# A fused transformer block on one core: first keys gathered in halves by two queues, x loaded first, the value bias moved into the residual, and no score maxima for a fifth chunk

## The chip, the cores and the metric

The kernel runs on one core of one Trainium2 chip. Its engines are TensorE (PE; PEld is its weight load), VectorE (DVE), ScalarE (ACT), GpSimd (POOL) and SyncE (SP); a name with a q behind it (SPq, ACTq) is that engine's queue of instructions, from which it also issues DMAs. The metric is device time in microseconds (us), the median of several executions.

## The reference

```python
x = x + cross_attention(layernorm(x), ctx, ctx, tau, delta)   # softmax(E**-0.5 * (q k^T tau + delta_s)) v, 16 heads of E = 16
x = x + expert_ffn(layernorm(x))                              # 8 experts, the best one by the router, times its probability
x = x + window_attention(ctx, layernorm(x), len, p_t)         # keys p_t - 16 .. p_t + 16, gauss weights, tanh(cat @ W_c^T)
x = x + slot_layer(layernorm(x))                              # top 8 of 64 slots per token, GRU and attention over the slots
```

x has 2048 tokens of 256 channels, ctx has 1601 rows of 256. Queries, keys, values and the output of the first attention are projections of 256 by 256 with a bias each: q = Wq x + bq, k = Wk c + bk, v = Wv c + bv, and the result is out @ Wo^T + bo. Everything is float32.

## The kernel before

The tokens are worked off in 4 chunks (`NC`) of 512 (`CT`). The 16 heads form 4 groups (`NG`) of 4 (`HG`), the 1601 context rows 13 tiles (`ST`).

**The stacks.** Scores come from one bf16 product over 101 rows: q and k are each split into three bf16 parts whose products are stacked over 6 times 16 rows (`PART_OF_ROW`), three rows carry the three parts of delta against ones, and two rows carry the negated maximum of each token against ones. The parts are made in blocks of 128 channels by up to 512 columns (`BLOCKS`: `("K", i, m)`, `("Q", i, m)`). For a block, PE projects (`project`, L829), ACT writes the float32 copy (L666) and the high part (L672), and the first 6 blocks are then split on DVE (`split`, L1220, L1222, L1224), the later ones by POOL and ACT (L606, L678, L613). SP's queue then gathers the stack rows: `gather_k(g)` moves 6 times 16 partitions of 4 heads by 1601 columns (L473), `first_q(g)` the same for q (L482).

**Three stretches.** (1) `START`: loads, K blocks 0 to 3 of the first 128 channels, both Q blocks of chunk 0, and 8 of the 13 value tiles (`V`, L904 on PE, L1254 on DVE, which adds the bias bv). The normalised x that the Q blocks need comes from `stats` on DVE, `scale_shift` on POOL (L580 to L590) and L697 on ACT. (2) `UNITS + LEAD` = 78 maximum units, with the remaining blocks laid between them by the list `BESIDE` (pairs of a unit's number and a step, the same list walked by every engine). A unit is one product of 99 rows by 401 columns (`max_unit`, L869) and one DVE maximum over it (`take_max`, L1292); 64 units give the maxima of one group of heads for one chunk. Three PSUM banks (`RING`) hold units in flight. (3) Four chunks of 52 slots (`SLOTS`), a slot being one tile of context rows for one group of heads: 4 score products (L1152), 4 exponentials on ACT (L719), 4 value products (`pv`, L948), and 4 or 5 maximum units for what comes 78 units later. Everything else of the previous chunk (`behind(c - 1)`: output projection, experts, window attention, slots) is laid between the slots by a fixed table of places (`AT`). After the last slot `behind(3)` and the slot layer run alone.

In the fourth chunk the units of the third stretch run on past the last group: units 1024 to 1101 are maxima for a fifth chunk, from queries that SP has copied behind the stored ones:

```python
sp.dma_start(q_parts[:, :, T:T + CT], q_parts[:, :, 0:CT]).then_inc(s["q0_copied"], 16)
```

The maxima come into the query stack as two rows (`load_m`, L492). For the first group SP issues them behind all the query stores:

```python
for i in range(1, NC):
    for m in range(KT):
        store_q(i, m)
wait_taken(sp, "m", 0)
load_m(0)
```

In each chunk `chunk_loads` lets SP load the next maxima and queries, and, in its fourth step, store the previous chunk's residual and load x for this chunk into `xres` (L547), to which POOL adds the bias bo (L639).

## Time and profile before

| | us |
|---|---|
| median of 3 runs (lowest, highest) | 1152.18 (1151.59, 1152.73) |
| the profiled execution's own time | 1152.93 |
| its span in the profile | 1151.2 |
| PE busy, share of the span | 1017.0, 88% |
| DVE busy | 790.4, 69% |
| ACT busy | 576.1, 50% |
| first maximum unit starts on PE | 48.28 |
| first score product of the third stretch | 119.95 |
| last score product | 1012.52 |

Busy time is a union: a matmul counts from its start to its modelled end, so matmuls that overlap are counted once, and a PE busy all the time isn't a PE at its peak. In the rows, `out<-in` names the tensors; the brackets at the end of a timeline row give the idle time of the engine before it and what ended it. Where a tensor shares the memory of another, the profile uses the other's name (`q_stack<-q_stack` is the split of delta, `expert_w` holds the projection weights early on, `xres` the ones).

### The profile page before, as it was taken

The page shows a single profiled execution, that of the slowest core. Times are in us where ns is not written, and L with a number is a line of the kernel's source. Part 1 is how long each engine was busy: PE and PEld are TensorE (multiplying, and loading weights), DVE is VectorE, ACT ScalarE, POOL GpSimd, SP SyncE. Part 2 cuts the span into 40 slices and gives each one's busy share as a digit, 9 for nine tenths or more (in the row PEclk, how much of TensorE's full clock was granted, in tenths as well). Part 3 has the DMA queues.
Part 4 walks back from the last instruction along what each step waited for, and adds up shares of the span by engine and source line. Part 5 has one row for each costly group of instructions (what it writes and reads, how often), then busy time and mean ns, then how long its engine had stood idle before and what let it go on. Part 6 is the DMA issues. An engine that isn't in the chain of part 4 may idle for free.

```text
span 1151.2 us, 13842 instructions
## 1 busy us (share of the span) xinstructions
PE 1017.0 (88%) x4890; PEld 410.2 (36%) x4890; DVE 790.4 (69%) x1772; ACT 576.1 (50%) x1047; POOL 68.3 (6%) x86
## 2 busy tenths in 40 slices
PE   5677899999899998989889999888999989889887
PEld 2333222222333333433333334323333334344544
DVE  3487678788766778676777767776677787735444
ACT  4144566666544556665445546664444465720120
POOL 5143000000100000000000000001000000010000
PEclk8889899999989999999899989999999899999999
DMA  4981700000100000001000000010000000050022
GB/s 127 154 167 56 170 15 1 15 15 3 30 1 15 1 15 1 15 1 52 1 15 1 14 1 15 1 38 14 15 1 3 12 1 15 1 165 1 1 91 73
DMA packets 35746, 38.28 MB, mean 33 GB/s; under 512 B 6943, under 2 KB 32320, under 8 KB 35416
## 3 DMA queue, kind: packets, MB, share of 16 engines
q1 hardware_dynamic: 34988, 36.83, 13.0%
q8 instruction: 39, 0.64, 0.2%
q0 software_dynamic: 80, 0.26, 0.2%
q10 hardware_dynamic: 608, 0.30, 0.1%
q14 instruction: 31, 0.25, 0.1%
HBM read 23.49 MB, written 8.13 MB: 27 GB/s over the span
## 4 chain that ended last, share of the span: by engine, by line
issue 45%; PE 30%; DVE 11%; DMA 4%; ACT 3%; SPq 3%; DVEq 2%; POOL 2%; POOLq 1%; ACTq 0%
PE ps_o L948 8%; PE ps_e L1152 8%; PE ps_m L869 7%; DVE mx L1292 6%; DMA xres<-in_x 1%; SPq L436 1%; PE ps_e L829 1%; ACT probs L719 1%; PE ps_m L1096 1%; PE ps_m L1099 1%; DMA x<-xres 1%; POOL xres L639 1%; DVE xn L1284 1%; POOL rstd L582 1%; PE ps_m L1003 1%
## 5 line engine op out<-in xcount | busy, mean ns | idle before, releaser
L1292 DVE TENSOR_REDUCE mx<-ps_m 128x1 f32<-128x401 f32 x1102 | 580.6, 568 | 235.6 <-PE ps_m L869 227.7
L719 ACT ACTIVATE probs<-ps_e 128x512 f32<-128x512 f32 (+1 forms) x832 | 472.7, 597 | 374.2 <-PE ps_e L1152 373.2
L869 PE MATMUL ps_m<-k_stack,q_stack 99*128 99x401 bf16 x1102 | 343.8, 344 | 50.6 <-DVE mx L1292 41.2
L1152 PE MATMUL ps_e<-q_stack,k_stack 101*128 101x512 bf16 (+1 forms) x832 | 327.1, 393 | 14.9 <-DMA q_stack<-mrow 6.6
L948 PE MATMUL ps_o<-probs,v_heads 128*32 128x512 f32 (+1 forms) x1664 | 228.4, 622 | 0.0
L1152 PEld LDWEIGHTS ps_e<-q_stack,k_stack 101*128 101x128 bf16 (+1 forms) x832 | 82.8, 100 | 310.2 <-ACT probs L719 205.4
L869 PEld LDWEIGHTS ps_m<-k_stack,q_stack 99*128 99x128 bf16 x1102 | 110.2, 100 | 177.0 <-DVE mx L1292 112.8
L1046 PE MATMUL ps_m<-expert_w,xnT 128*128 128x512 f32 x256 | 130.1, 609 | 16.3 <-DVE xb L1428 16.3
L1428 DVE SCALAR_TENSOR_TENSOR xb<-ps_m,hot,xb 128x256 f32<-128x256 f32 x112 | 54.2, 484 | 18.0 <-PE ps_m L1046 9.0
L1046 PEld LDWEIGHTS ps_m<-expert_w,xnT 128*128 128x128 f32 x256 | 47.1, 194 | 47.9 <-DVE xb L1428 24.7
L948 PEld LDWEIGHTS ps_o<-probs,v_heads 128*32 128x32 f32 (+1 forms) x1664 | 33.2, 109 | 65.7 <-issue 57.3
L580 POOL TENSOR_TENSOR var_e<-mv,eps 128x4 f32<-128x4 f32 x16 | 3.2, 200 | 654.6 <-DVE mv L1377 647.1
L729 ACT COPY xnT<-ps_m 128x512 f32<-128x512 f32 x24 | 13.8, 587 | 48.1 <-PE ps_m L993 48.1
L968 PE MATMUL ps_m<-wc,ident 128*128 128x512 f32 x64 | 29.6, 602 | 0.8 <-ACT alphaT L788 0.8
L639 POOL TENSOR_TENSOR xres<-xres,bo 128x1024 f32<-128x1024 f32 x4 | 9.4, 2356 | 312.2 <-DMA xres<-in_x 312.2
L829 PE MATMUL ps_e<-probs,expert_w 128*128 128x512 f32 (+1 forms) x32 | 19.0, 722 | 7.9 <-DMA probs<-in_ctxT 7.9
L829 PE MATMUL ps_e<-xnT,expert_w 128*128 128x512 f32 x32 | 20.9, 759 | 1.7 <-issue 1.7
L1096 PE MATMUL ps_m<-win_v,work 128*128 128x256 f32 x64 | 19.6, 399 | 2.0 <-ACT work L729 2.0
L993 PE MATMUL ps_m<-ident,xn 128*128 128x128 f32 x96 | 18.5, 291 | 2.9 <-DVE xn L1284 2.7
L666 ACT ACTIVATE work<-ps_e,cond 128x512 f32<-128x512 f32 (+1 forms) x8 | 4.7, 592 | 29.5 <-PE ps_e L829 29.5
L1099 PE MATMUL ps_m<-wc,xnT 128*128 128x256 f32 x64 | 19.3, 394 | 0.0
L666 ACT ACTIVATE work<-ps_e,cond,tau 128x512 f32<-128x512 f32 x8 | 6.2, 778 | 24.0 <-PE ps_e L829 24.0
(236 smaller groups left out, 650.6 us busy)
## 6 DMA issues: line engine op xcount, KB each, us to landing
q_stack<-q_parts SPq DMA_DIRECT2D x96, 64.0 KB, 2.5
k_stack<-k_stack SPq DMA_DIRECT2D x12, 200.1 KB, 8.6
expert_w<-in_expert_wT SPq DMA_DIRECT2D x2, 1024.0 KB, 10.5
xres<-in_x SPq DMA_DIRECT2D x4, 512.0 KB, 3.9
x<-xres SPq DMA_DIRECT2D x4, 512.0 KB, 3.2
probs<-x SPq DMA_DIRECT2D x1, 2048.0 KB, 8.3
out<-probs SPq DMA_DIRECT2D x4, 512.0 KB, 3.0
k_stack<-alphaT SPq DMA_DIRECT2D x10, 200.1 KB, 8.1
```

The costliest lines, as they stand in the source:

```text
L639: pool.tensor_tensor(xres[:], xres[:], bo0[:].unsqueeze(1).broadcast_to((P, TT, D)), ALU.add)\
L719: act.activation(probs[0:n, k % 2, h, :], ps_e[h % 2][0:n, :], ACT.Exp).then_inc(s["exp_done"], 1)
L829: mm = pe.matmul(ps_e[b % 2][:, 0:n], wqkv[:, w, k, P * m:P * m + P], src[:, k, at_col:at_col + n], start=(k == 0), stop=(k == KT - 1))
L869: pe.matmul(ps_m[:, (UNITS * n1 + u) % RING, 0:SPLIT], qst[0:MAX_ROW, g, h, P * t:P * t + P], kst[0:MAX_ROW, HG * g + h, QUARTER_START[q]: ...
L948: mm = pe.matmul(ps_o[32 * h:32 * h + 32, :], v_sb[0:n, st, HG * g + h, :], probs[0:n, k % 2, h, :], start=(st == 0), stop=(st == ST - 1))
L968: pe.matmul(out, ident[:], wc[:, 0:KT, :], start=True, stop=True)
L1046: mm = pe.matmul(bank(name, c), xnT[:, k, P * t:P * t + P], expert_w[:, k, CT * j:CT * j + CT], start=(k == 0), stop=(k == KT - 1))
L1096: pe.matmul(o, aT[:, k, tok:tok + P], win_v[:, k, :], start=(k == 0), stop=False)
L1099: mm = pe.matmul(o, xnT[:, k, tok:tok + P], wc[:, KT + k, :], start=False, stop=(k == KT - 1))
L1152: pe.matmul(ps_e[h % 2][0:n, :], kst[0:ROWS, HG * g + h, P * st:P * st + n], qst[0:ROWS, g, h, :], start=True, stop=True).then_inc(s["qk_r ...
L1292: dve.tensor_reduce(mx[:, q, col:col + 1], ps_m[:, (UNITS * n1 + u) % RING, 0:SPLIT], AX.X, ALU.max)\
L1428: last = dve.scalar_tensor_tensor(out=xb[:, t, :], in0=bank(f"e{i}", c)[:, D * (e % 2):D * (e % 2) + D], scalar=hot8[:, t, e:e + 1], in1=( ...
```

## The change

- **Loads.** x's first chunk goes first on SP's queue, Wq third, x's second chunk before all waits. The bias bv is no longer loaded; Wo comes with the constants.
- **Delta.** It is laid out over 13 partitions of 128 and split by DVE. The three parts go out to memory and come back spread over 12 heads in one DMA; the ones come in 2 DMAs in place of 6.
- **Order of the start.** DVE takes x's statistics before the conditions, POOL the scale and shift before its window load. Ten products of ones run on PE ahead of everything (`WARM`). tau is multiplied into Wq (`S`), no longer applied by ACT. `("Q", 0, 1)` and three value tiles move from `START` to `BESIDE`, whose pieces lie 2 units apart in place of 2.4 and number 36 in place of 31.
- **Gathers.** The first group's keys move in two halves of columns, each when its blocks are split, rows 0, 4, 2 by SP and rows 1, 5, 3 by ACT; its queries likewise. The gathers of groups 2 and 3 both come behind all query stores.
- **Early split.** For the first 5 blocks DVE reads PSUM itself and adds the bias; ACT's float32 copy is left out.
- **Values.** ACT copies the value tiles. PE forms bv @ Wo^T in 4 matmuls on a broadcast bv, and DVE adds that to bo.
- **Maxima.** `load_m(0)` is issued by ACT. Units from 1024 on, their transposes, the copy of the queries, and the loads of queries for a fifth chunk are left out. `xres` is loaded after the store of the previous chunk's residual without waiting for the maxima of a group 16, but with a wait until its last readers on DVE are through.

```diff
-EARLY = N_COLS + 2
-V_EARLY = 8
-START = [("D",), ("C",), ("L", 0), ("K", 0, 0), ("K", 1, 0), ("N", 0), ("K", 2, 0), ("T", 0), ("K", 3, 0), ("Q", 0, 0), ("Q", 0, 1)]
+EARLY = N_COLS + 1
+V_EARLY = 5
+HALVES = ((0, 2 * CT, 1), (2 * CT, S, N_COLS - 1))
+GATHER_SP, GATHER_ACT = (0, 4, 2), (1, 5, 3)
+START = [("D",), ("L", 0), ("C",), ("K", 0, 0), ("N", 0), ("S",), ("K", 1, 0), ("T", 0), ("K", 2, 0), ("K", 3, 0), ("G", 0),
+         ("Q", 0, 0), ("G", 1), ("g",)]
...
+SPACE = 2
+WARM = 10
...
-BESIDE += [(76, ("P", "Q", 3, 1))]
+BESIDE += [(SPACE * len(PIECES) + 2, ("P", "Q", 3, 1)), (UNITS + 8, ("m",))]
...
+def wanted(n1):
+    return n1 < NG * NC
...
+            sp.dma_start(xa[:], x_dram[:, 0:TT, :]).then_inc(x_start[0], 16)
             load_w(0, "L0_WkT")
             load_ctx(0)
-            sp.dma_start(xa[:], x_dram[:, 0:TT, :]).then_inc(x_start[0], 16)
...
+            sp.dma_start(d_parts.rearrange("a (p s) -> p a s", s=P), delta3[:]).then_inc(s["delta_stored"], 16)
+            sp.wait_ge(s["delta_stored"], 16)
+            sp.dma_start(kst[DELTA_ROW:DELTA_ROW + 3, 0:3 * HG, :], d_parts[:, 0:S].unsqueeze(1).broadcast_to((3, 3 * HG, S)))\
+              .then_inc(s["ld_delta_k"], 16)
...
-            gather_k(0)
-            sp.wait_ge(s["ld_delta_k"], 48)
-            first_q(0)
-            sp.dma_start(xb[:], x_dram[:, TT:2 * TT, :]).then_inc(x_start[1], 16)
+            rows = range(K_PARTS)
+            for first_col, end_col, last_block in HALVES:
+                sp.wait_ge(s["blk_parts"], BLOCK["K", last_block, 0] + 1)
+                move_k(sp, 0, GATHER_SP, first_col, end_col)
+            sp.wait_ge(s["blk_parts"], BLOCK["Q", 0, 0] + 1)
+            move_q(sp, 0, GATHER_SP)
+            move_q(sp, 1, rows)
+            store_q(0, 0)
...
-            wait_taken(sp, "m", 0)
-            load_m(0)
+            move_k(sp, 2, rows)
...
                 for g in range(NG):
-                    wait_taken(sp, "m", NG * c + g + 1)
-                    load_m((g + 1) % NG)
-                    load_q(sp, (g + 3) % NG, c if g == 0 else c + 1)
-                    if g == NG - 1:
-                        if behind:
-                            store_x3(c - 1)
-                            sp.wait_ge(s["x3_stored"], 16 * c)
-
-                        sp.dma_start(xres[:], x_dram[:, c * TT:c * TT + TT, :]).then_inc(s["x_loaded"], 16)
+                    if wanted(NG * c + g + 1):
+                        wait_taken(sp, "m", NG * c + g + 1)
+                        load_m(sp, (g + 1) % NG)
+                    if g == 0 or c < NC - 1:
+                        load_q(sp, (g + 3) % NG, c if g == 0 else c + 1)
+                if behind:
+                    store_x3(c - 1)
+                    sp.wait_ge(s["x3_stored"], 16 * c)
+                    sp.wait_ge(s["xn_ready"], NC + 3 * c)
+                sp.dma_start(xres[:], x_dram[:, c * TT:c * TT + TT, :]).then_inc(s["x_loaded"], 16)
...
-            pool.wait_ge(s["delta_hi"], 1)
-            pool.tensor_tensor(delta_b, delta_a, delta3[:, 0, :], ALU.subtract)
...
+                if b >= EARLY:
+                    act.wait_ge(s["blk_rest"], b - 1)
+                    act.activation(q32[:, b % 2, 0:n], ps_e[b % 2][:, 0:n], ACT.Identity, bias=bias)
...
+                if kind == "m":
+                    wait_taken(act, "m", 0)
+                    load_m(act, 0)
...
+                    for k in range(KT):
+                        mm = pe.matmul(ps_x[:, W:W + D], bv_rows[:, k, :], wo_rows[:, k, :], start=(k == 0), stop=(k == KT - 1))
...
                         for j, u in units_at(k, h):
-                            max_unit(u, c, j)
+                            if wanted(NG * c + j):
+                                max_unit(u, c, j)
```

## Rows read from the trace of the kernel before

**Rows 1.** Stretches: start:end length, busy PE PEld DVE ACT POOL, clock, DMA share, GB/s
```profile
0.00:48.20 48.20, 24.90 (x64) 14.06 (x64) 19.56 (x47) 14.45 (x20) 17.19 (x21) 0.88 0.66 120
48.20:114.40 66.20, 50.33 (x183) 25.71 (x183) 51.45 (x122) 27.47 (x46) 25.27 (x34) 0.88 0.58 131
...
944.20:1013.50 69.30, 62.76 (x348) 25.95 (x348) 51.20 (x122) 43.60 (x78) 1.21 (x2) 1.00 0.04 10
```
**Rows 2.** Timeline of the start: start us, us, engine line operation
```profile
6.62 3.75 PE L829 MATMUL ps_e<-probs,expert_w 128*128 128x512 f32 x4 [6.62 <-DMA probs<-in_ctxT]
17.97 0.19 POOL L580 TENSOR_TENSOR var_e<-mv,eps 128x4 f32<-128x4 f32 x1 [5.75 <-issue]
25.46 3.28 POOL L625 TENSOR_TENSOR q_stack<-expert_w,q_stack 16x1601 bf16<-16x1601 f32 x1
31.13 4.59 SPq L473 DMA_DIRECT2D k_stack<-k_stack  x6
35.85 4.31 SPq L482 DMA_DIRECT2D q_stack<-probs  x6
48.28 0.50 PE L869 MATMUL ps_m<-k_stack,q_stack 99*128 99x401 bf16 x1 [8.07 <-DMA q_stack<-probs]
```
**Rows 3.** Timeline of early blocks: DVE's operations, one of them slow, and ACT's norm
```profile
11.77 0.69 DVE L1220 TENSOR_TENSOR work<-work,k_stack 128x512 f32<-128x512 f32 x1 [0.35 <-ACT k_stack L672]
12.55 0.43 DVE L1222 CAST k_stack<-work 128x512 bf16<-128x512 f32 x1
13.05 0.69 DVE L1224 TENSOR_TENSOR k_stack<-work,k_stack 128x512 bf16<-128x512 f32 x1
20.74 2.07 ACT L697 ACTIVATE xn<-xa,off,rstd 128x256 f32<-128x256 f32 x4 [3.99 <-POOL off L590]
25.95 3.07 DVE L1222 CAST k_stack<-work 128x512 bf16<-128x512 f32 x1
```
**Rows 4.** Stretches by DMA rate, the last column: first gather, constants
```profile
36.00:40.00 4.00, 4.00 (x20) 3.36 (x18) 1.86 (x5) 0.00 (x0) 0.00 (x0) 1.00 1.06 116
48.00:52.00 4.00, 3.72 (x7) 1.76 (x8) 1.63 (x3) 0.00 (x0) 0.00 (x0) 0.50 1.10 342
```
**Rows 5.** Groups of instructions from 48.2 to 114.4 us, PE and DVE
```profile
L904 PE MATMUL ps_o<-expert_w,probs 128*128 128x256 f32 (+1 forms) x20 | 5.3, 385 | 0.0
L1254 DVE TENSOR_TENSOR v_heads<-ps_o,scratch 128x256 f32<-128x256 f32 (+1 forms) x5 | 2.1, 413 | 0.0
```
**Rows 6.** Timeline between the last of the 78 units and the first score product
```profile
117.03 1.21 SPq L492 DMA_DIRECT2D q_stack<-mrow  x2
119.95 0.58 PE L1152 MATMUL ps_e<-q_stack,k_stack 101*128 101x512 bf16 x1 [6.63 <-DMA q_stack<-mrow]
```
**Rows 7.** The maximum products among the groups from 944.2 to 1013.5 us
```profile
L869 PE MATMUL ps_m<-k_stack,q_stack 99*128 99x401 bf16 x79 | 24.3, 336 | 4.2 <-DVE mx L1292 4.1
```
**Rows 8.** Timeline of PE in one slot of chunk 0
```profile
224.19 0.51 PE L869 MATMUL ps_m<-k_stack,q_stack 99*128 99x401 bf16 x2
225.20 0.39 PE L1152 MATMUL ps_e<-q_stack,k_stack 101*128 101x512 bf16 x1
225.69 1.07 PE L948 MATMUL ps_o<-probs,v_heads 128*32 128x512 f32 x8
```
**Rows 9.** Stretches within the last 16 slots
```profile
947.90:966.60 18.70, 18.29 (x104) 9.66 (x103) 11.38 (x22) 10.75 (x19) 0.00 (x0) 1.00 0.09 22
966.60:982.30 15.70, 13.88 (x78) 4.83 (x77) 14.06 (x35) 9.49 (x18) 1.21 (x2) 1.00 0.00 1
993.50:1013.50 20.00, 16.96 (x89) 5.01 (x91) 15.87 (x45) 11.93 (x25) 0.00 (x0) 1.00 0.06 12
```
**Rows 10.** Timeline behind the last slot: x and the first residual
```profile
1017.82 0.38 SPq L547 DMA_DIRECT2D xres<-in_x  x1
1019.47 3.69 PE L1003 MATMUL ps_m<-wo_rows,attn_chunk 128*128 128x256 f32 x16 [0.77 <-ACT attn_chunk L729]
1021.79 2.35 POOL L639 TENSOR_TENSOR xres<-xres,bo 128x1024 f32<-128x1024 f32 x1 [44.87 <-DMA xres<-in_x]
```

More of the change, by code:

```diff
@@ L156, in job_numbers @@
                 order += [(name, c - 1) for name in AT if AT[name] == q]
-            if q in M_AT:
+            if q in M_AT and wanted(NG * c + 1 + M_AT.index(q)):
                 order.append(("m", NG * c + 1 + M_AT.index(q)))
@@ L429, in block_cols, with k_loads, move_k, move_q @@
             return k_cols[BLOCKS[b][1]][1] if BLOCKS[b][0] == "K" else CT
+        def k_loads(g):
+            return K_PARTS * (2 if g == 0 else 1) + (g == 3)
+        def move_k(eng, g, rows, first_col=0, end_col=S):
+            m, first = g * HG // (P // E), g * HG % (P // E)
+            for j in rows:
+                eng.dma_start(kst[16 * j:16 * j + 16, HG * g:HG * g + HG, first_col:end_col],
+                              k_part[m][PART_OF_ROW[j]][E * first:E * (first + HG), first_col:end_col]).then_inc(k_loaded[g], 16)
+        def move_q(eng, g, rows):
+            m, first = g * HG // (P // E), g * HG % (P // E)
+            for j in rows:
+                part = [a for start, a, copies in PART_GROUPS for _ in range(copies)][j]
+                eng.dma_start(qst[16 * j:16 * j + 16, g, :, :], q_part[m][E * first:E * (first + HG), part, :])\
+                   .then_inc(q_loaded[g], 16)
+        def load_m(eng, g):
+            for a in range(2):
+                eng.dma_start(qst[MAX_ROW + a:MAX_ROW + a + 1, g, :, :], mrow[:, a, :]).then_inc(m_loaded[g], 16)
         def load_q(eng, g, chunk):
@@ L476, in first_q @@
-            def first_q(g):
-                m, first = g * HG // (P // E), g * HG % (P // E)
-                sp.wait_ge(s["blk_parts"], BLOCK["Q", 0, m] + 1)
-                for j, a, copies in PART_GROUPS:
-                    for i in range(copies):
-                        sp.dma_start(qst[16 * (j + i):16 * (j + i) + 16, g, :, :], q_part[m][E * first:E * (first + HG), a, :])\
-                          .then_inc(q_loaded[g], 16)
+            sp.dma_start(d_parts.rearrange("a (p s) -> p a s", s=P), delta3[:]).then_inc(s["delta_stored"], 16)
@@ L501, in _ @@
                 sp.dma_start(dst, src).then_inc(s["ld_const"], 16)
-            gather_k(1)
-            first_q(1)
-            first_q(2)
-            for m in range(KT):
-                store_q(0, m)
+            store_q(0, 1)
+            move_q(sp, 2, rows)
+            move_k(sp, 1, rows)
             sp.wait_ge(s["xnT_ready"], 2)
             sp.dma_start(xb[:], x_dram[:, 3 * TT:4 * TT, :]).then_inc(x_start[1], 16)
-            gather_k(2)
             for i in range(1, NC):
@@ L662, in block_hi @@
                 n = block_cols(b)
-                bias, scale = (qk_bias[:, 1, :], 1.0) if kind == "K" else (qk_bias[:, 0, :], tau[:, 2:3])
+                bias = qk_bias[:, kind == "K", m:m + 1]
                 act.wait_ge(s["blk_psum"], b + 1)
-                need(act, s["blk_rest"], b - 1)
-                act.activation(q32[:, b % 2, 0:n], ps_e[b % 2][:, 0:n], ACT.Identity, bias=bias[:, m:m + 1], scale=scale)
+                if b >= EARLY:
+                    act.wait_ge(s["blk_rest"], b - 1)
+                    act.activation(q32[:, b % 2, 0:n], ps_e[b % 2][:, 0:n], ACT.Identity, bias=bias)
                 if kind == "Q":
@@ L920, in _ @@
             under_way = []
+            pe.wait_ge(s["consts_set"], 1)
+            for _ in range(WARM):
+                pe.matmul(ps_o[:], ones_sb[:, 0:P], ones_sb[:, 0:CT], start=True, stop=True)
             for now in START:
                 if now == ("T", 0):
-                    pe.wait_ge(s["ld_early"], 32)
+                    pe.wait_ge(s["ld_early"], 16)
                 step(*now)
                 finish()
-            pe.wait_ge(s["ld_k"], 32)
-            pe.wait_ge(s["ld_delta_k"], 48)
-            pe.wait_ge(s["ld_ones"], 16 * NG)
+            pe.wait_ge(s["ld_k"], 16)
+            pe.wait_ge(s["ld_delta_k"], 16)
+            pe.wait_ge(s["ld_ones"], 16)
             pe.wait_ge(s["v_taken"], V_EARLY)
@@ L1316, in step @@
                     stats((xa, xb)[i % 2])
[L1317 to L1321 removed]
+                if kind == "D":
+                    split_delta()
                 if kind == "C":
                     condition()
+                if kind == "S":
+                    dve.wait_ge(w_loaded[2], 16)
+                    dve.tensor_scalar(wqkv[:, 2], wqkv[:, 2], tau[:, 2:3], None, ALU.mult).then_inc(s["wq_scaled"], 1)
                 if kind == "U":
@@ L1532, in chunk @@
                         go_on(work, HG * k + h)
-                        if h == 2 and max_end(k - 1) is not None:
+                        if h == 2 and max_end(k - 1) is not None and wanted(NG * c + max_end(k - 1)):
                             j = max_end(k - 1)
```

163 lines of the change are left out of this document (83 added, 80 removed), and 8 rows, old and new, of the table PIECES.

## The prediction

> **What bounds the kernel now.** I read the table of stretches first, cut where the work changes [rows 1]. The first 48.2 us feed PE for 24.9 us only: nothing of the main work has begun. From 48.2 to 114.4 neither engine is full: PE is busy 50.3 us of 66.2, DVE 51.5, and they wait for each other through three PSUM banks. From 114.4 to 119.9 PE does nothing [rows 6]. Then come four chunks of slots, of which the diff alters only the last 16 slots, from 944.2 to 1013.5 us, where PE is busy 62.8 us of 69.3. Behind them runs a serial end. So four places count: when the first maximum unit can start, how long the 78 units take, the hole behind them, and the last 16 slots with what follows.
>
> The timeline of the start shows what the first unit (48.28) waited for [rows 2]. SP gathers the keys only from 31.13, after POOL's last delta part (25.46 + 3.28 = 28.74) and three DMAs for it; six key DMAs take 4.59 us to issue, six query DMAs end their issue at 35.85 + 4.31 = 40.16, and PE is released by the last query landing, 8 us later. That is no latency but a backlog: while it lasts the DMA share is full (1.06), yet only 116 GB/s move, against 342 when constants come from memory [rows 4].
>
> **Part 1, the start.** x (512 KB) goes ahead of Wk and the first context columns. At 342 GB/s it costs 1.5 us, so the first K block starts near 8.2 instead of 6.62 [rows 2, 4]. The ten products of ones lie before it, in PE's idle time; whether they make the first block's 3.75 us into half I can't see in this trace, and it matters by 1.9 us at most. x itself is there some 3 us sooner, and POOL takes its scale and shift before its window load. With statistics ending near 8.5 and a POOL chain of 2.8 us (17.97 to 20.74, [rows 2, 3]), ACT's normalisation (2.07 us) ends near 13.4 where it ended at 22.8 [rows 3].
>
> From there DVE paces. A block costs it 0.69 + 0.43 + 0.69 us and two drains, 2.05 us [rows 3]. The third block's cast took 3.07 us instead of 0.43 while POOL worked on delta [rows 2, 3]; with delta in 13 partitions on DVE that overlap is gone. ACT spends one pass per block, not two. I lay it out: K block 0 split by 12.9, K block 1 by 16.3 (ACT gives it the high part after the normalisation), block 2 by 19.1, the short block 3 by 19.9, the query block by 22.3. SP, which had waited for delta's round trip through memory behind 3.4 MB of loads (about 16 to 17 us at 342 GB/s, [rows 4]), issues the first key half from about 17.2, the second from 19.9, its query rows from 22.3 to 24.2; ACT does the same with 1 us delay. tau into Wq is one DVE pass below 0.7 us, before K block 1 has its high part.
>
> The gathers move 1.2 MB of keys and 0.4 MB of queries, with delta 1.74 MB. At the 116 GB/s of [rows 4] this takes 15.0 us from 17.2: 32.2, and with the landing and group 1's queries, which share the engines, 33.5. If the two queues get more out of the DMA engines, the limit is the last issue at 24.2 plus 2.2 to 2.9 us: 27. SP and ACT take row groups 16 partitions apart, which spreads the writes; but the nearest row is the slow one, so I take 31. That is 17.3 us before 48.28 [rows 2].
>
> The Trainium skill says otherwise (DMA: Bandwidth & Descriptors, section "Issuing engines are not separate DMA queues"): DMAs of several issuers interleave on the same 16 engines, and a second issuer saves only the time of issuing. By it the first unit would start near 33.5. No run here shows two queues gathering at once.
>
> **Part 2, the 78 units.** Added on PE: one query block, half of the 3.75 us of [rows 2] at the higher clock, 1.9; three value tiles, 1.06 each by 5.3 / 5 [rows 5]; four small products for bv @ Wo, 0.9. Together 6.0 us. Off DVE go five value additions, 2.1 us [rows 5]; on it come a broadcast copy and one addition, 0.8. ACT takes eight value copies, about 0.4 us each; it is busy 27.5 us of 66.2 [rows 1], which hides them. The normalisations are asked for 7 units ahead of their transposes, not 4; I credit 4 us of PE's idle time for that, of 15.9 us (66.2 - 50.3) in all. Of the 6.0 us added, part falls into gaps of PE: the stretch goes from 66.2 to 68 us, with bounds of 62 (all hidden, waits gone) and 73 (all added, nothing gained). It ends at 31 + 68 = 99.
>
> **Part 3, the hole.** PE's first score product waits 6.63 us for the rows of maxima, which SP issues at 117.03 behind the last query store [rows 6]. ACT will issue them right after its last high part, before the last split. Left are two issues of 0.6 us and 1.7 to 2.2 us of landing from about the 73rd unit on, that is 1 to 1.5 us behind the last unit. The third stretch starts near 100.2 instead of 119.95: 19.7 us saved. What is late next is nothing I can find. Groups 2 and 3 of the keys are now gathered behind all query stores, 12 DMAs at 4.59 us per six [rows 2], landed by about 125; the first unit that reads group 2 is the 50th of the third stretch, at 4 to 5 units per slot its tenth slot, beyond 130. ACT's exponentials wait for the split and the last store of channel half 0, as now.
>
> **Part 4, the last 16 slots.** 78 units go, with one turn of maxima. On PE the 79 products show 24.3 us busy [rows 7], which is the upper bound. But products overlap: two in a row show 0.51 us, one 0.34 [rows 7, 8], so one more costs 0.17, and 78 cost 13.3. The lower bound is the one unit that lies between a slot's last score product and its value products: 0.49 us between their starts, 0.22 left without it [rows 8], 0.27 x 16 = 4.3, if ACT's exponentials and the two banks hold everything else in place. By parts [rows 9]: 947.9 to 966.6 is PE-bound (18.29 of 18.7), some 20 units less, 3.4 us. 966.6 to 982.3 is DVE-bound (14.06 of 15.7); without its maxima DVE has some 3.5 us of work there, PE 13.88 - 3.4 = 10.5, ACT 9.5: 3.1 us. 993.5 to 1013.5: PE 16.96 - 3.6, ACT 11.9: 2.6 us. The other 14.9 us (69.3 less these three) hold ACT's table loads around the gelu: 2.1 us for 17 units. Sum 11.2 us.
>
> **Part 5, behind the last slot.** x for chunk 3 is issued at 1017.82, behind the useless maxima and queries of a fifth chunk, POOL adds bo from 1021.79 to 1024.14, while PE has both halves of the projection done at 1023.16 [rows 10]. With the load issued after the previous residual's store, tens of us earlier, DVE begins at the first half and ends its second addition near 23.8 instead of 25.45: 1.7 us, carried through, for the chain behind is serial. The new wait for the residual's readers is over in every chunk before its x is wanted.
>
> **Sum.** 19.7 + 11.2 + 1.7 = 32.6 us. From the span of 1151.2 to 1118.6, from the execution's own 1152.93 to 1120.3; it lies 0.75 above the median of the runs, so 1119.6.
>
> **The rivals.**
> - *One rate for both queues* (by the rule above): the gathers stay at 116 GB/s and the first unit waits to 33.5. For it: the full share at 116 GB/s in [rows 4]. Against: the share says busy engines, not used ones. 2.5 us more: 1122.1. Chance 0.25.
> - *Freed PE time isn't usable.* The last slots keep their pace because exponential and score product alternate on two banks; 4.3 us in place of 11.2, and the 78 units take 73: 1119.6 + 6.9 + 5 = 1131.5. For it: ACT idles in those slots waiting for PE, and PE for it. Chance 0.13.
> - *The maximum units cost what they show.* 24.3 us in the last slots, 1106.5. Against: the overlap in [rows 8]. For it: DVE is the pace of two of the parts [rows 9]. Chance 0.1.
> - *Slower: the clock.* With a third of PE's work gone in the last 16 slots the granted clock could fall from 1.00 there [rows 1] to half and stay. PE's 62.8 - 13.3 = 49.5 us would become 99 us, 29.7 more than the 69.3 now, 41 more than forecast: 1160. It decides only if nearly all 16 slots run at half, from about 33 us of extra time on. Against: in the 78-unit stretch PE is busy 76% and still has 0.88, and [rows 9] shows 1.00 at 85%. Chance 0.02.
> - *The edits buy nothing*, because another wait stands in the same places (SP behind delta's round trip until the old time, 31.13, and a late group 2): about 1150. Chance 0.01.
>
> **How the numbers follow.** The forecast, 1119.6, has 0.49. Its own range is 1115 to 1124: the start of the first unit between 27 and 33.5, the units between 65 and 71. The range to give reaches to the neighbours: 1108 to 1130 leaves out the worst of the second rival, the full price of the third, and the last two. Faster by over 0.2% (2.3 us, about what a measurement of this kernel can tell from no change): 0.97. Within: 0.01. Slower: 0.02.
>
> **What would show it.** First maximum unit at 27 to 34 us, with a DMA rate in the gather above or at 116 GB/s; K block 1 split by 16 to 17; normalised x near 13. 78 units in 62 to 73 us. The first score product within 2 us of the last unit's end. Slots of the last quarter at about 3.6 us in place of 4.3, the clock still 1.00. x's load for chunk 3 before 1000 us, and no wait for POOL behind the last slot. The prediction is wrong if the start is held by a DMA that I haven't counted (delta and ones now lie on few partitions and so on few DMA engines), if the units need over 73 us, or if the last slots gain less than 5 us.

## The result, and the profile after

| | before | after |
|---|---|---|
| median, us (lowest to highest, 4 runs each) | 1152.31 (1151.59 to 1152.73) | 1119.32 (1118.38 to 1120.53) |
| ratio after / before, 95% interval | | 0.9729 [0.9697, 0.9761] |
| the profiled execution's own time | 1152.93 | 1120.53 |
| its span | 1151.2 | 1118.8 |
| first maximum unit on PE | 48.28 | 35.81 |
| first score product of the third stretch | 119.95 | 98.07 |
| PE busy | 1017.0 | 1008.3 |

The change takes 33 us off, 2.7%, which is what was forecast. The profile says that two of the terms were nevertheless wrong, in opposite directions. To see it, cut the execution after at the same events as before and read the stretches; columns as in [rows 1]. Later on, "the last 16 slots" runs from the first exponential of slot 36 of the fourth chunk to the end of the last exponential: 944.2 to 1013.5 before [rows 1], 920.4 to 983.1 after.

```profile
0.00:35.80 35.80, 22.55 (x60) 11.44 (x60) 12.78 (x40) 9.38 (x18) 8.91 (x18) 0.92 0.85 181
35.80:97.60 61.80, 51.91 (x201) 28.68 (x201) 49.03 (x117) 31.17 (x58) 27.58 (x37) 0.93 0.45 111
...
920.40:983.10 62.70, 55.73 (x269) 19.89 (x271) 11.35 (x42) 42.94 (x79) 3.56 (x3) 0.86 0.06 18
98.50:920.40 821.90, 762.87 (x3900) 280.02 (x3899) 611.32 (x1329) 469.82 (x862) 16.88 (x20) 0.97 0.07 17
983.10:1118.80 135.70, 114.69 (x400) 63.17 (x392) 56.63 (x153) 20.09 (x42) 4.42 (x8) 0.95 0.19 60
```

Lined up with the forecast (minus is time saved, in us of the span; "before" takes the first exponential at 120.6 as the end of the start, "after" at 98.5):

| stretch | forecast | profile after | from |
|---|---|---|---|
| start, units and hole, up to the third stretch | -19.7 | -22.1 | 120.6 to 98.5 |
| the first 192 slots | 0 | -1.7 | 823.6 to 821.9 |
| the last 16 slots | -11.2 | -6.6 | 69.3 to 62.7 |
| behind them | -1.7 | -2.0 | 137.7 to 135.7 |
| sum | -32.6 | -32.4 | 1151.2 to 1118.8 |

**The start.** The timeline of the changed kernel (PE, DVE, ACT and the two queues):

```profile
2.81 4.44 PE L957 MATMUL ps_o<-xres 16*128 16x512 bf16 x10 [2.81 <-POOL xres L589]
8.74 5.89 PE L861 MATMUL ps_e<-probs,expert_w 128*128 128x512 f32 x8 [1.49 <-DMA probs<-in_ctxT]
...
12.60 0.69 ACT L683 ACTIVATE k_stack<-ps_e,cond 128x512 bf16<-128x512 f32 x1 [7.69 <-PE ps_e L861]
...
13.19 2.06 ACT L728 ACTIVATE xn<-xa,off,rstd 128x256 f32<-128x256 f32 x4
...
14.67 0.69 DVE L1264 TENSOR_TENSOR k_stack<-work,k_stack 128x512 bf16<-128x512 f32 x1
...
17.20 0.69 DVE L1264 TENSOR_TENSOR k_stack<-work,k_stack 128x512 bf16<-128x512 f32 x1
...
18.30 0.24 SPq L503 DMA_DIRECT2D k_stack<-d_parts  x1
...
18.59 5.37 SPq L451 DMA_DIRECT2D k_stack<-k_stack  x6
19.33 1.84 ACTq L451 DMA_DIRECT2D k_stack<-k_stack  x2
...
19.83 1.96 PE L861 MATMUL ps_e<-xnT,expert_w 128*128 128x512 f32 x4 [1.26 <-DVE work L1259]
...
24.61 6.09 SPq L459 DMA_DIRECT2D q_stack<-probs  x9
...
35.81 0.52 PE L901 MATMUL ps_m<-k_stack,q_stack 99*128 99x401 bf16 x1 [3.24 <-DMA q_stack<-probs]
```

Normalised x is there by 13.19 + 2.06 = 15.3 (forecast 13.4, before 22.8): ACT makes the high part of K block 0 first, and for that it waits until 12.60 for PE. K block 1 is split at 17.9 (forecast 16.3), the first half is issued at 18.6 (17.2), right behind the DMA of delta's rows, whose way through memory had held SP until 18.3, the queries at 24.6 (22.3), and PE is still released by a query row, 11.2 us after that issue. The stretches by DMA rate show what lies between:

```profile
8.00:12.00 4.00, 3.25 (x4) 1.51 (x5) 1.54 (x17) 0.00 (x0) 1.82 (x5) 1.00 1.08 375
...
20.00:24.00 4.00, 4.00 (x16) 2.77 (x15) 2.81 (x8) 0.69 (x1) 0.00 (x0) 1.00 1.07 146
24.00:28.00 4.00, 1.03 (x4) 0.59 (x3) 0.58 (x1) 0.93 (x3) 0.00 (x0) 0.86 1.08 131
28.00:32.00 4.00, 3.28 (x10) 2.21 (x8) 0.00 (x0) 0.74 (x2) 0.00 (x0) 0.72 1.15 145
32.00:36.00 4.00, 0.76 (x3) 0.13 (x2) 0.00 (x0) 0.00 (x0) 0.00 (x0) 0.71 1.13 209
```

Loads from memory move 375 GB/s (first row). The share is as full afterwards, but 131 to 146 GB/s move while the first group's rows are on their way, little more than the 116 of [rows 4]; the 209 of the last row already hold loads from memory again.

**The hole.** ACT issues the rows of maxima before the last unit, and PE waits 0.34 us where it waited 6.63 [rows 6]:

```profile
94.47 0.58 ACTq L464 DMA_DIRECT2D q_stack<-mrow  x1
95.08 0.61 ACTq L464 DMA_DIRECT2D q_stack<-mrow  x1
...
98.07 0.38 PE L1189 MATMUL ps_e<-q_stack,k_stack 101*128 101x512 bf16 x1 [0.34 <-DMA q_stack<-mrow]
```

**The last 16 slots.** In the stretches above PE's clock is 0.86 there, where [rows 1] had 1.00. Finer stretches show where it goes:

```profile
956.00:960.00 4.00, 3.80 (x20) 1.64 (x20) 0.00 (x0) 3.46 (x5) 0.00 (x0) 1.00 0.00 0
960.00:962.00 2.00, 1.04 (x8) 0.97 (x8) 0.00 (x0) 1.97 (x3) 0.00 (x0) 1.00 0.03 8
962.00:966.00 4.00, 3.19 (x12) 0.54 (x12) 2.75 (x16) 2.38 (x5) 0.00 (x0) 0.51 0.00 0
...
974.00:978.00 4.00, 3.68 (x14) 0.83 (x14) 0.42 (x1) 2.17 (x4) 0.00 (x0) 0.50 0.00 0
978.00:982.00 4.00, 4.00 (x17) 0.90 (x9) 0.00 (x0) 1.52 (x3) 0.00 (x0) 0.85 0.00 0
```

From 962.5 to 979.5 the granted clock is 0.50, the lower of its two levels, 1.2 GHz. What PE did before: at 960 to 962 it was busy half of the time, behind ACT's table loads for the gelu. Slots 47 to 51, from 962.2 on, take 20.9 us against 20.0 before, although they have lost their units; the eleven slots ahead of them take 41.8 against 49.3. That is the rival of the clock, in small.

**Behind them.** x for chunk 3 is loaded at 947.5 and has its bias long before DVE wants it at 991, so no wait for POOL is left:

```profile
947.52 0.37 SPq L564 DMA_DIRECT2D xres<-in_x  x1
951.30 2.35 POOL L650 TENSOR_TENSOR xres<-xres,bo 128x1024 f32<-128x1024 f32 x1 [5.29 <-DMA xres<-in_x]
...
988.92 3.69 PE L1040 MATMUL ps_m<-wo_rows,attn_chunk 128*128 128x256 f32 x16 [0.77 <-ACT attn_chunk L760]
990.99 0.69 DVE L1409 TENSOR_TENSOR xa<-xres,ps_m 128x512 f32<-128x512 f32 x1 [3.99 <-PE ps_m L1040]
992.65 0.69 DVE L1409 TENSOR_TENSOR xa<-xres,ps_m 128x512 f32<-128x512 f32 x1 [0.97 <-PE ps_m L1040]
```

### The profile page after: what moved, and what is told of

Read it like the earlier page. It is cut to its first block, busy times and chain, and to the rows that moved or that the text cites. A ratio compares the mean times of both kernels' runs of the same rounds, so it can differ in the third digit from the quotient of the medians.

```text
span 1118.8 us, 13600 instructions
## 1 busy us (share of the span) xinstructions
PE 1008.3 (90%) x4825; PEld 403.5 (36%) x4825; DVE 742.0 (66%) x1681; ACT 573.4 (51%) x1056; POOL 62.3 (6%) x85
## 4 chain that ended last, share of the span: by engine, by line
issue 52%; PE 28%; DVE 9%; DMA 4%; ACT 2%; POOL 2%; DVEq 2%; SPq 1%; POOLq 0%; ACTq 0%
PE ps_e L1189 7%; PE ps_o L985 7%; PE ps_m L901 6%; DVE mx L1335 4%; PE ps_e L861 2%; DMA xres<-in_x 1%; SPq L471 1%; POOL rstd L599 1%; DMA q_stack<-probs 1%; POOL xres L650 1%; ACT probs L750 1%; DVE xn L1327 1%; PE ps_m L1133 1%; PE ps_m L1136 1%; PE ps_m L1248 1%
## 5 line engine op out<-in xcount | busy, mean ns | idle before, releaser
L1335 DVE TENSOR_REDUCE mx<-ps_m 128x1 f32<-128x401 f32 x1024 | 539.4, 569 | 212.3 <-PE ps_m L901 204.1
L901 PE MATMUL ps_m<-k_stack,q_stack 99*128 99x401 bf16 x1024 | 319.1, 343 | 34.4 <-DVE mx L1335 29.7
L985 PE MATMUL ps_o<-probs,v_heads 128*32 128x512 f32 (+1 forms) x1664 | 231.7, 630 | 0.0
L901 PEld LDWEIGHTS ps_m<-k_stack,q_stack 99*128 99x128 bf16 x1024 | 102.3, 100 | 150.8 <-DVE mx L1335 90.9
L1083 PE MATMUL ps_m<-expert_w,xnT 128*128 128x512 f32 x256 | 129.1, 605 | 16.3 <-DVE xb L1472 16.3
L1083 PEld LDWEIGHTS ps_m<-expert_w,xnT 128*128 128x128 f32 x256 | 46.7, 193 | 47.4 <-DVE xb L1472 24.7
L1519 DVE TENSOR_TENSOR xres<-xb,work 128x512 f32<-128x512 f32 x8 | 5.5, 687 | 22.4 <-ACT work L803 22.4
L677 ACT ACTIVATE work<-ps_e,cond 128x512 f32<-128x512 f32 (+1 forms) x11 | 7.2, 653 | 22.2 <-PE ps_e L861 22.2
L1040 PE MATMUL ps_m<-win_k,xnT 128*128 128x256 f32 x64 | 16.2, 383 | 2.2 <-issue 1.4
```

The source lines that it names most:

```text
L901: pe.matmul(ps_m[:, (UNITS * n1 + u) % RING, 0:SPLIT], qst[0:MAX_ROW, g, h, P * t:P * t + P], kst[0:MAX_ROW, HG * g + h, QUARTER_START[q]: ...
L985: mm = pe.matmul(ps_o[32 * h:32 * h + 32, :], v_sb[0:n, st, HG * g + h, :], probs[0:n, k % 2, h, :], start=(st == 0), stop=(st == ST - 1))
L1083: mm = pe.matmul(bank(name, c), xnT[:, k, P * t:P * t + P], expert_w[:, k, CT * j:CT * j + CT], start=(k == 0), stop=(k == KT - 1))
L1335: dve.tensor_reduce(mx[:, q, col:col + 1], ps_m[:, (UNITS * n1 + u) % RING, 0:SPLIT], AX.X, ALU.max)\
```

## The experiments

Each kernel is the changed kernel with the edit shown, run beside the kernel before on the same chip, on one of two chips. Times spread more there: the kernel before took 1144.3 to 1156.5, and the changed kernel, on one of them, 1114.6 to 1121.2. So times are read as ratios to before with their intervals, and most verdicts rest on stretches of the profile. The changed kernel's own ratio is 0.9729 [0.9697, 0.9761] above and 0.9735 [0.9709, 0.9762] in a second measurement there (its profile is read further down). Each edit has one profile. What two profiles of the same work can differ by is seen in those whose edit leaves a stretch alone: the first unit comes between 35.3 and 37.1 us, and the 78 units take 58.2 to 63.5 us from the first one's start to the last one's.

**The fifth chunk's maxima put back.**

```diff
 def wanted(n1):
-    return n1 < NG * NC
+    return True
```

with the queries for them and their waits.

> The changed kernel with the 78 maximum units for a fifth chunk, their transposes and query loads put back (the queries are read from chunk 0's own place, no copy). It prices the removal alone. In the profiles the last 16 slots went from 68.8 to 62.2 us between exponentials and what follows them from 138.2 to 136.2. If that difference is the removal's, this kernel needs 8.6 us more than the changed one, about 1128, its last 16 slots take 68 to 69 us, the granted clock there stays at 1.00, and POOL waits again for the last x behind the last slot. Rival: half of the 8.6 us comes from another part of the change (the start leaving the chunks in another phase); then this kernel gains less than 5 us.

Measured: 1126.52 us, ratio 0.9782 [0.973, 0.9835]. The last 16 slots take 69.5 us, as before, at a clock of 1.00. Behind them it is 140.3 us, where the two profiles of the changed kernel have 135.7 and 137.0. So this one edit of the many is worth 6.8 us in the slots by the first profile of the changed kernel, 10.6 by the second (58.9 us, below). The load of x is issued behind the last slot again, but DVE's first addition is then released by PE, not by POOL. By the two ratios the whole costs 5 to 6 us; the intervals overlap, so the time alone proves no size.

**PE keeps its products, DVE is spared the maxima.** Each unit of the fifth chunk but the last still issues its product, on old queries, into the same banks; nothing reads it.

```diff
                             if wanted(NG * c + j):
                                 max_unit(u, c, j)
+                            elif (k, h) != (SLOTS - 1, HG - 1):
+                                fill_unit(u, c, j)
```

> The changed kernel with PE's 77 products of the removed units kept, without waits and without DVE's maxima. In the changed kernel the granted clock is 0.5 from 962 to 979 us and slots 47 to 50 take 4.3 us each, against 3.1 to 4.0 before. Theory: PE had too little to do, the clock fell, and that cost some 6 us. Then here the clock stays at 1.00, the last 5 slots take about 3.2 us each instead of 4.3, and the products cost the first 11 slots up to their 0.17 us each, 7 to 9 us: total between 1118 and 1123. Rival: the slow slots come from the alternation of score product and exponential on two banks, not from the clock; then the slots stay at 4.3 us or more and the total is 1126 or more.

Measured: 1126.08 us, ratio 0.9802 [0.9736, 0.9869], with 1122.95 in the profiled execution. The stretch of its last 16 slots, and below it that of the second profile of the changed kernel:

```profile
922.90:987.30 64.40, 61.60 (x346) 25.41 (x348) 11.36 (x42) 43.38 (x79) 3.57 (x3) 1.00 0.06 17
```

```profile
918.20:977.10 58.90, 51.21 (x269) 19.69 (x271) 11.45 (x42) 43.03 (x79) 3.56 (x3) 0.97 0.06 19
```

The maxima on DVE, with PE's waits for them (4.1 us in [rows 7]), were worth 69.3 - 64.4 = 4.9 us, the products on PE another 64.4 - 58.9 = 5.5. DVE lost 40 us of work and PE only 10; both count, because in parts of this stretch DVE had been the pace [rows 9]. With the products kept, the clock stays at 1.00 throughout, and slots 47 to 51 take 17.0 us. That is the theory's mark, and the rival's slow slots don't appear; the time of 1126 is the rival's figure all the same. In the profile the products cost more than the clock gives back: the eleven slots ahead take 47.4 us, against 41.8.

**Spare products in the gap of the gelu.** In the fourth chunk PE runs two spare products where it otherwise waits for ACT's table loads.

```diff
                 yield AT["logits"]
+                if c == NC - 2:
+                    pe.wait_ge(s["max_taken"], UNITS * NG * NC)
+                    keep_warm(2, ps_m[:, 0, :])
                 wait_taken(pe, "h", c)
```

> The changed kernel with two spare products of 512 columns (0.88 us each) on PE just before it waits for the gelu of chunk 2, where PE stands idle 1.2 us while ACT loads its tables. Theory: this gap tips the clock; filled, the clock stays at 1.00 to the end of the slots, slots 47 to 50 take about 3 us and not 4.3, and the whole takes 5 to 6 us less: 1113.5. Rival: PE's work in those slots is too thin anyway, the clock falls a little later, and the gain is under 2 us.

Measured: 1117.29 us, ratio 0.97 [0.9646, 0.9753]. The stretch is 57.6 us at a clock of 1.00:

```profile
924.30:981.90 57.60, 51.19 (x273) 20.41 (x275) 11.39 (x42) 43.04 (x79) 3.56 (x3) 1.00 0.06 19
```

So the fall starts in that gap. The time is 3 to 4 us lower by the ratios, where the theory expected 5 to 6, and the intervals overlap. At this point I took the fall for a property of the changed kernel, worth 5 us.

**The changed kernel once more**, with no edit, to test that.

> The changed kernel once more, unchanged. In its first profile the granted clock was at half from 962.5 to 979.5 us and the last 16 slots took 62.2 us; in the kernels without the warm products, with the second group later, with SP's maxima and with DVE's values it fell there for 3.4 us only and they took 58.2 to 58.6. Theory A (which of the two happens depends on where the clock's periods lie in an execution, not on the kernel's work): a second profile can show either; if it shows a fall of 3.4 us, the last 16 slots take 58.3. Theory B (it belongs to this kernel's own work): again 17 us at half and 62. Time by either within 0.3% of 1119.3.

Measured: 1115.76 us, ratio 0.9735 [0.9709, 0.9762]. The same work takes 58.9 us in the second profile (the row above) where it took 62.7 in the first, and the clock is low for one short period only:

```profile
956.00:960.00 4.00, 2.79 (x19) 1.24 (x18) 0.02 (x1) 3.90 (x5) 0.00 (x0) 1.00 0.02 4
960.00:964.00 4.00, 3.25 (x11) 0.53 (x12) 2.74 (x16) 2.33 (x5) 0.00 (x0) 0.61 0.00 0
964.00:968.00 4.00, 2.91 (x15) 0.52 (x13) 0.00 (x0) 2.87 (x6) 0.00 (x0) 0.96 0.00 0
968.00:972.00 4.00, 3.40 (x15) 0.87 (x16) 1.45 (x4) 3.94 (x11) 0.00 (x0) 1.00 0.00 0
```

The same instructions, the same gap, another outcome: theory A. Of the seven other kernels here that leave these slots as they are, six show 58.8 to 59.2 us for the stretch and one 62.9. The Trainium skill (TensorE: Matmul & The Clock Gate, section "What's actually happening") says that the chip watches PE's activity on a clock of its own which the kernel doesn't start, so that the same kernel shows different patterns. It says so of a kernel's first products; the two profiles agree and show it far into the kernel, 62.7 against 58.9 us.

**One queue for the gather.**

```diff
-GATHER_SP, GATHER_ACT = (0, 4, 2), (1, 5, 3)
+GATHER_SP, GATHER_ACT = (0, 1, 2, 3, 4, 5), ()
```

> The changed kernel with the first group's keys and queries all issued by SP, still in halves. The gathers moved about 140 GB/s with two queues, 116 before with one. Theory A (two queues raise the rate by spreading the writes): the rate falls to about 116 GB/s and the first maximum unit comes 2 to 3 us later than 35.8. Theory B (the first unit waits because group 1's queries and a store, issued by SP right behind, share the engines with ACT's last query rows): with one queue in order the first group's rows land ahead of them and the first unit comes no later, perhaps 1 to 2 us earlier. Total: A 1121.5, B 1118 to 1119.5.

Measured: 1119.05 us, ratio 0.9729 [0.9679, 0.9779]. First unit at 35.13 with one queue, 35.81 and 36.8 in the two profiles with two:

```profile
24.00:28.00 4.00, 2.57 (x11) 1.63 (x9) 0.79 (x2) 1.67 (x5) 0.00 (x0) 1.00 1.09 131
28.00:32.00 4.00, 1.10 (x2) 0.30 (x2) 0.00 (x0) 0.00 (x0) 0.00 (x0) 1.00 1.02 139
```

131 and 139 GB/s with a full share, as with two, and a first unit no later: theory A falls. The second queue brings nothing. The Trainium skill (DMA: Bandwidth & Descriptors, section "Issuing engines are not separate DMA queues") says that a second issuing engine saves only the time of issuing; the trace agrees, 131 and 139 GB/s with one queue against 131 and 145 with two. The issues themselves do take longer, 15.4 us in a row from 18.5 to 33.9 by SP alone, but that queue isn't what is waited for.

**No warm-up.**

```diff
-WARM = 10
+WARM = 0
```

> The changed kernel without the ten products of ones (WARM 0). In the changed kernel they ran from 2.8 to 7.2 us, and the first key products behind them, from 8.74, still took about 0.85 us each until 13.6. Theory A (they bring nothing in this place: the clock of the first key block is the same without them): first maximum unit within 0.5 us of 35.8, time within 1.5 us of the changed kernel's 1119.3. Theory B (without them PE stays at the lower clock through the second key block too, so that both halves of the keys come later): first unit 2 to 4 us later, 1121.5 to 1123.

Measured: 1115.98 us, ratio 0.9686 [0.963, 0.9741], first unit at 35.86. The first key products:

```profile
8.74 5.28 PE L861 MATMUL ps_e<-probs,expert_w 128*128 128x512 f32 x8 [8.74 <-DMA probs<-in_ctxT]
```

They start at the same moment, and eight of them take 5.28 us (5.09 in the version at the end, also without the ten products), where the eleven profiles with them show 5.08 to 6.69, 5.89 and 5.33 in the two of the changed kernel. So the warm-up brings nothing that can be seen here. Both ways the products start at half speed: four of them take some 3.75 us, the four of the query block 1.96 at 19.83. The column of the granted clock reads 1.00 in the first stretches even so (8 to 12 us above), so it doesn't show this slow start; that it is the clock is read from the times alone. The time lies 3.3 us below the 1119.3 of theory A; by the ratios the intervals overlap.

**The second group's queries later.** SP issues them only when the first group's have landed.

```diff
             move_q(sp, 0, GATHER_SP)
+            sp.wait_ge(q_loaded[0], 96)
             move_q(sp, 1, rows)
```

> The changed kernel with one wait more: SP issues the second group's queries only once all six rows of the first group's queries have landed. Theory A (the first unit waits for a backlog on the DMA engines, of which the second group's 0.4 MB is a part): at 131 to 145 GB/s they take 2.7 to 3 us of the engines; not all of it lies ahead of the first group's last row, so the first unit comes 1 to 3 us sooner, at 33 to 35, and the time is 1116.5 to 1118.5. Theory B (the last row is as late by its own packets): first unit unchanged at 35.8, and the second group's queries, now 2 to 3 us later, are wanted only at the 65th unit: no change of the time beyond 1 us.

Measured: 1119.27 us, ratio 0.9723 [0.966, 0.9786], first unit at 35.38. Theory B. The rate shows why less traffic doesn't help:

```profile
28.00:32.00 4.00, 3.28 (x9) 2.14 (x8) 0.00 (x0) 0.74 (x2) 0.00 (x0) 0.50 1.11 126
32.00:36.00 4.00, 2.50 (x4) 0.75 (x5) 0.06 (x1) 0.00 (x0) 0.00 (x0) 0.50 0.16 29
```

From 32 to 36 us the share is 0.16, some 2.6 of the 16 DMA engines, and 29 GB/s move; the unit waits until 35.4 all the same. In the trace's DMA records pieces of the first group's own rows still move until 35.0, of its keys (1154 bytes each) until 33.6, so the last rows sit with a few engines while the others have nothing to do. The pieces as long as delta's rows (3202 bytes) end by 24.8, by 23.9 in the changed kernel: delta and the ones, which lie on few partitions, aren't what the unit waits for.

**Both halves late.** The first half waits for the fourth block, as one gather of the whole would.

```diff
-HALVES = ((0, 2 * CT, 1), (2 * CT, S, N_COLS - 1))
+HALVES = ((0, 2 * CT, N_COLS - 1), (2 * CT, S, N_COLS - 1))
```

> The changed kernel with both halves of the first keys gathered only when the fourth key block is split (21.8 us), as one gather of the whole would be; the DMAs are the same ones. Theory A (the keys' DMAs run at the limit of their DMA engines from 18.6 us on, and a later start moves the end by as much): first unit 3 to 3.5 us later, at 39, time 1122 to 1123. Theory B (the first unit waits for the query rows' own path from their issue at 24.6, with what is ahead of them in the engines of little weight): first unit at 36 to 37, time within 1.5 us of 1119.3.

Measured: 1115.04 us, ratio 0.9715 [0.969, 0.974]. The keys are issued from 21.75, 3.2 us later, yet:

```profile
21.75 5.27 SPq L451 DMA_DIRECT2D k_stack<-k_stack  x6
...
27.26 6.76 SPq L459 DMA_DIRECT2D q_stack<-probs  x9
...
36.82 0.52 PE L901 MATMUL ps_m<-k_stack,q_stack 99*128 99x401 bf16 x2 [0.44 <-DMA q_stack<-probs]
```

The first unit comes at 36.8, as in the second profile of the changed kernel (36.8) and 1 us behind the first. Moving the first half early, the edit in the change's name, is worth at most 1 us there. Theory A expected 39 and falls. Nor is that 1 us left later on: the first score product comes at 95.67, 2.4 us ahead of the changed kernel's 98.07, since the units take 58.2 us in place of 61.6 here; they begin at the higher clock (1.00 in the row below, 0.50 in the same 4 us of the changed kernel).

```profile
36.00:40.00 4.00, 3.56 (x14) 1.97 (x14) 2.50 (x5) 1.58 (x3) 0.35 (x1) 1.00 1.10 281
```

**The first rows of maxima by SP.**

```diff
             for i in range(1, NC):
                 for m in range(KT):
                     store_q(i, m)
+            wait_taken(sp, "m", 0)
+            load_m(sp, 0)
             move_k(sp, 2, rows)
```

and ACT's two issues away.

> The changed kernel with one undo: SP, not ACT, issues the first rows of maxima, behind the last query store. Theory A (the hole of 6.6 us in the kernel before came from where these two DMAs stood in the queue): the hole between the last of the 78 units and the first exponential grows from 1.1 us to 5 to 7, time 1123 to 1125. Theory B (most of the hole went because the blocks ahead of it now end sooner, and the queue no longer matters): hole at most 2.5 us, time within 1.5 us of 1119.3.

Measured: 1121.87 us, ratio 0.9746 [0.9691, 0.9802]:

```profile
99.09 1.23 SPq L464 DMA_DIRECT2D q_stack<-mrow  x2
```

```profile
101.66 0.58 PE L1190 MATMUL ps_e<-q_stack,k_stack 101*128 101x512 bf16 x1 [3.94 <-DMA q_stack<-mrow]
```

A wait of 3.94 us instead of 0.34: 3.6 us, between the theories' sizes and clearly a wait behind the last store. The hole before was 6.63 us, so about half of it was the queue's order. The rest went because the last query store comes sooner relative to the units: SP's two DMAs are issued 1.4 us behind the end of the last unit (99.09, and 101.66 - 3.94 = 97.7), before it was 3.7 (117.03, and 119.95 - 6.63 = 113.3 [rows 6]).

**Value tiles by DVE.**

```diff
 # in DVE's step, and ACT's take_v away
+                    dve.tensor_copy(v_sb[0:n, st, :, 0:E], v_psum(st).rearrange("p (h e) -> p h e", h=H)).then_inc(s["v_taken"], 1)
```

> The changed kernel with the value tiles copied out of PSUM by DVE, as before (without the bias), not by ACT. Theory A (the 78 units went from 64.6 to 61.6 us, with 6 us more for PE in them, because DVE lost its value additions): eight copies of 0.4 us on DVE give back about 3 us, 78 units in 64 to 65.5 us, time 1121.5 to 1123. Theory B (the units are paced by PE and its waits, and what took the stretch from the predicted 68 to 62 us is the order of the steps, above all the normalisations asked for earlier): 78 units within 1 us of 61.6, time within 1.5 us of 1119.3.

Measured: 1121.16 us, ratio 0.9741 [0.9682, 0.9801]. The 78 units:

```profile
36.70:102.00 65.30, 54.08 (x201) 29.11 (x201) 51.94 (x125) 28.61 (x50) 27.28 (x36) 0.91 0.43 102
```

From the first unit's start to the last one's it is 65.3 us, against 61.6 and 61.1 in the two profiles of the changed kernel: DVE is busy 2.9 us longer and the stretch is 3.7 to 4.2 us longer. Theory A, though the size is uncertain: the largest of the profiles that leave the units alone is 63.5.

**Normalisations asked for later.**

```diff
-            BESIDE += [(max(SPACE * i - 15, 0), ("L", step[1])), (SPACE * i - 7, ("N", step[1]))]
+            BESIDE += [(max(SPACE * i - 11, 0), ("L", step[1])), (SPACE * i - 4, ("N", step[1]))]
```

> The changed kernel with statistics and normalisations asked for 11 and 4 units ahead of their transposes, as before, in place of 15 and 7. Theory A (most of what the 78 units gained over the predicted 68 us comes from here: PE no longer waits for normalised x): 78 units take 3 to 5 us more than 61.6, time 1122 to 1124. Theory B (the gain is DVE's and the overlap of the added products with gaps): 78 units within 1 us of 61.6, time within 1.5 us.

Measured: 1128.04 us, ratio 0.9819 [0.9786, 0.9852], the only undo whose interval lies wholly above the changed kernel's. The changed kernel took 1115.76 on the same chip. The units take 66.1 us, 4.5 to 5.0 more, and PE shows the waits that the wider distance had removed:

```profile
58.84 1.97 PE L927 MATMUL ps_m<-ident,xn 128*128 128x128 f32 x8 [3.41 <-ACT xn L728]
...
74.52 1.09 PE L927 MATMUL ps_m<-ident,xn 128*128 128x128 f32 x8 [1.66 <-ACT xn L728]
```

The two rows show 5.1 us of waiting, and eight transposes that take 1.97 us instead of 1.09, at the lower clock from 58.5 to 65.3. Theory A. Its profiled execution took 1120.96 us, the others 1126 to 1131; what those 5 us more are, no profile shows.

**A version meant to be faster**: no warm-up, and the spare products at the gelu.

> A version meant to be faster: the changed kernel without the ten products of ones, and with two rounds of spare products on PE ahead of the logits in the fourth chunk's hidden layer, where PE otherwise waits for ACT's table loads. Theory A (the gap tips the clock, in some executions for 17 us): it takes 0 to 5 us less than the changed kernel in the last 16 slots, which take 57, clock 1.00 through slot 46, and the time is 1 to 4 us below the same chip's run of the changed kernel. Theory B (a fall there costs nothing that isn't given back in the tail): no difference beyond 0.5 us.

Measured: 1115.82 us, ratio 0.973 [0.9702, 0.9758], beside 1115.76 for the changed kernel. The last 16 slots take 57.6 us at a clock of 1.00, 1.3 less than in the usual case of the changed kernel, and nothing of it is left in the time, as theory B has it. Its executions range from 1111.6 to 1122.2, so a gain of 1 us couldn't be seen. Neither kernel beats the other.

## Why the prediction came out right

**The parts that held.** The two places of the sum, the start and the last slots, are where the time went. The rows of maxima had been late behind a query store (Part 3): the wait went from 6.63 to 0.34 us, and back to 3.94 with SP issuing them. x's late load (Part 5): forecast 1.7 us; from the end of the last exponential to the end of the residual's second addition it was 1025.45 - 1013.5 = 11.95 us, now 993.34 - 983.1 = 10.2. The chain behind varies by more with the clock's periods (134.0 to 140.3 us over all runs), so the -2.0 of the table is no measure of it.

**Part 1 was mis-sized by 4.8 us.** The first unit came at 35.8, not 31, outside the 27 to 33.5 that I had given. Some 2.3 us are lateness ahead of the gathers: my times for the blocks took for granted that the warm-up makes K block 0's four products into half, but they took the 3.75 us of [rows 2] again, and they began at 8.74, not 8.2. So its split ended at 15.4 where I had 12.9, and the query block's 2.3 us later than laid out. Delta's way through memory ended at 18.3; the 16 to 17 us that I gave it don't follow from 3.4 MB at 342 GB/s either, which are 9.9 us. The other 2.5 lie in the gather: I had taken a value between one and two queues' rates, and one queue gives the same 131 to 139 GB/s. The rival "one rate for both queues" was right as to the mechanism, but its own number, 33.5, was too early as well. What the runs add is that the total of bytes isn't the limit either: without the second group's queries, and with the first half 3.2 us later, the unit starts within about 1 us of where it did. Why the last rows are left with a few DMA engines is open; nothing was tried against it.

**Part 2 was mis-sized by 6.2 us, the other way.** The 78 units took 61.8 us to the end of the last, below my lower bound of 62, not 68. 1.1 of it is the stretch that I started from: it went to 114.4, while the last unit before ended at 113.3. The other 5 are real: a step of -3.2 us (from 65.0) in place of +1.8. I had credited 4 us to the earlier normalisations and let most of PE's 6.0 us of additions show. Undone alone, the normalisations cost 4.5 to 5.0 us, and the value copies 3.7 to 4.2, whose 2.1 us off DVE I had counted without giving them a time: with DVE busy 49 of 62 us and PE 52, what comes off DVE comes off the stretch. PE's idle time fell from 14.7 us (65.0 - 50.3) to 9.9 (61.8 - 51.9), and in it the waits for DVE's maxima from 9.2 to 2.6. That its busy time rose by 1.6 us only, not by 6.0, has two more reasons: two of the query block's four products ran ahead of the first unit, and the products of the key blocks took 6.1 us in place of 7.9, at a clock of 0.93 in place of 0.88.

**Part 4 was sized right, and the table's term isn't it.** 11.2 us were forecast. The second profile of the same kernel shows 69.3 - 58.9 = 10.4. The first shows 6.6, since the clock was low for 17 us, 3.8 us of loss. My rival named that mechanism and put it at 0.02, deciding only from 33 us of loss on; as a price of 0 to 4 us on a part of the executions it belonged in the sum, with about 1 us, since two of the nine profiles of these slots have it. What it takes is shown: with the products kept (two profiles) or the gap at the gelu filled (two) the clock stays at 1.00 in these slots, and in all nine without either it falls for 3.4 us at least. In the time of the whole, filling the gap shows no gain. The rival "freed PE time isn't usable" (4.3 us in place of 11.2) is refuted by the same row, and the full price of 24.3 as well.

**The first 192 slots** were given nothing and show 1.7 us less, 0.2% of the stretch; between two profiles of the changed kernel they differ by 2.7, so there is nothing to explain.

So the total was right because errors cancelled: up to the third stretch +4.8, -6.2 and a hole 0.7 us shorter than laid out make -2.1 at the first score product (98.07 for 100.2) and -2.4 at the first exponential, the first 192 slots -1.7, the end -0.3, and the last slots +4.6 in this profile. That the sum fits so closely is luck. The sizes of the edits, each undone alone and read from one profile each: normalisations and value copies some 4 to 5 us each in the units, the useless maxima 6.8 to 10.6 in the slots, SP's position of the first maxima 3.6, the early half at most 1, second queue and warm-up nothing. The 12.5 us at the first unit are then left to the rest of the start's edits (delta, x first, the shorter split); none of these was undone, so what each brings is not shown.

## What to carry to other kernels

Where the DMA engines are full at a low rate, as here, an earlier issue or a second issuing engine needn't bring the data sooner; look at what is waited for last. Where two engines keep pace with each other, take small work off the busier one and ask for late operands a few steps sooner: either paid more here than the transfers in the change's name. And profile the same kernel twice before a clock pattern is put down to an edit.

## What was unexpected of the hardware

- Two profiles of one kernel, same instructions: the granted clock at half for 17.0 us in the one and 3.4 us in the other behind the same gap, 62.7 against 58.9 us for the last 16 slots. A clock at half doesn't come back at once though PE is busy: 3.68 of 4 us from 966 to 978, still 0.50.
- Gathers from one part of the on-chip memory to another, in pieces of 16 partitions, moved 126 to 146 GB/s with a full DMA share, where loads from memory moved 375 (8 to 12 us) and 342 [rows 4].
- Ten products over 4.44 us, ended 1.5 us before the first key product, didn't speed it up: eight key products took 5.08 to 6.69 us in eleven profiles with them, 5.28 and 5.09 in two without, while the column of the granted clock read 1.00 for all of them.
